# Moving the first q of the second attention, and the weight splits behind it, into the block ahead of it

## The reference

```python
h   = layernorm(x) * (1 + ca) + sa
q_c = rmsnorm(h @ w_qa, g_qa)                    # 192 wide
q   = (q_c @ w_qb) -> 32 heads, q_nope 128 | q_rope 64
kv  = h @ w_kva;  k_c = rmsnorm(kv[:64], g_kva);  k_rope = kv[64:]
k_nope, v = k_c @ w_kvb                          # per head 128 | 128
q_rope, k_rope = rope(q_rope), rope(k_rope)      # a*cos + rotate_half(a)*sin
scores  = [q_nope|q_rope] . [k_nope|k_rope] * 192**-0.5
out     = softmax(scores) @ v;  x = x + ga * (out @ w_o)
```

## Time and profile before

| | |
|---|---|
| profiled execution, its own time | 926.43 us |
| its span (first to last instruction) | 924.3 us |
| median of three timed runs | 926.45 us |
| PE busy | 823.0 us, 89% of the span |
| DVE busy | 679.4 us, 74% |
| ACT busy | 534.9 us, 58% |
| POOL busy | 536.3 us, 58% |
| granted TensorE clock, mean | 0.963 of full |

### The profile page before, as it was taken

One profiled execution on the slowest core, in us unless ns is written; L12 is line 12 of the kernel. 1 busy time (PEld: TensorE's weight loads), 2 busy tenths in 40 slices (PEclk: granted clock), 3 DMA queues, 4 the chain that ended last, 5 costly groups with the idle time before them and its releaser, 6 DMA issues.

```text
span 924.3 us, 15057 instructions
## 1 busy us (share of the span) xinstructions
PE 823.0 (89%) x4560; PEld 543.3 (59%) x4560; DVE 679.4 (74%) x1321; ACT 534.9 (58%) x1157; POOL 536.3 (58%) x480
## 2 busy tenths in 40 slices
PE   3699996399997894799999999999999999999997
PEld 1478875387775772456556565656565656565443
DVE  3639888644543562989888989899998889898662
ACT  3667884533332772666666666666566666666522
POOL 1414432112132223898888888889788888887313
PEclk9989998699999895999999999999999999999999
DMA  8360000563434340466666666666567666666511
GB/s 327 123 232 2 1 2 2 173 170 116 141 104 126 111 152 12 101 162 147 161 148 158 149 158 150 160 147 154 131 151 184 179 152 153 154 154 148 127 39 68
DMA packets 91567, 120.84 MB, mean 131 GB/s; under 512 B 30368, under 2 KB 41632, under 8 KB 91488
## 3 DMA queue, kind: packets, MB, share of 16 engines
q1 hardware_dynamic: 66912, 86.31, 33.6%
q10 hardware_dynamic: 24576, 33.59, 14.8%
HBM read 42.22 MB, written 2.10 MB: 48 GB/s over the span
## 4 chain that ended last, share of the span: by engine, by line
PE 44%; DVE 9%; issue 5%; ACTq 2%; ACT 2%; POOL 1%; DMA 0%; POOLq 0%; DVEq 0%; SPq 0%
PE bank L1451 11%; PE bank L1438 6%; PE bank L1439 4%; PE bank L1440 4%; PE bank L1465 4%; PE bank L1466 3%; PE bank L1467 3%; PE bank L1509 3%; DVE blk L1569 2%; DVE cT_lo L1643 2%; ACTq L1380 2%; DVE stage_a L1545 1%; DVE nmax L1553 1%; PE bank L1424 1%; PE bank L1425 1%
## 5 line engine op out<-in xcount | busy, mean ns | idle before, releaser
L1553 DVE TENSOR_REDUCE nmax<-bank 128x1 f32<-128x512 f32 x256 | 174.1, 680 | 46.7 <-PE bank L1440 45.5
L1715 ACT ACTIVATE prob<-bank,nmax 128x512 f32<-128x512 f32 x172 | 118.2, 687 | 109.7 <-DVE nmax L1553 97.6
L1822 POOL TENSOR_TENSOR prob<-prob,rinv 128x512 f32<-128x512 f32 x129 | 132.5, 1041 | 37.0 <-DVE rinv L1561 35.7
L1438 PE MATMUL bank<-xk_hi,q_hi 128*128 128x512 f32 x256 | 113.4, 443 | 18.5 <-ACT prob L1715 9.6
L1569 DVE STREAM_TRANSPOSE blk<-prob 128x512 f32<-128x512 f32 x172 | 120.2, 699 | 6.9 <-ACT prob L1758 5.6
L1438 PEld LDWEIGHTS bank<-xk_hi,q_hi 128*128 128x128 f32 x256 | 48.4, 189 | 96.9 <-issue 52.2
L1439 PE MATMUL bank<-xk_lo,q_hi 128*128 128x512 f32 x256 | 101.9, 398 | 0.0
L1440 PE MATMUL bank<-xk_hi,q_lo 128*128 128x512 f32 x256 | 101.0, 395 | 0.0
L1817 POOL TENSOR_TENSOR q_lo<-stage_a,q_hi 128x512 fp32r<-128x512 f32 x64 | 82.1, 1283 | 28.2 <-ACT q_hi L1709 28.1
L1813 POOL TENSOR_TENSOR stage_a<-stage_a 128x512 f32<-128x512 f32 x64 | 82.7, 1293 | 7.0 <-DMA stage_a<-stage_a 6.2
L1715 ACT ACTIVATE stage_a<-bank,nmax 128x512 f32<-128x512 f32 x84 | 57.7, 687 | 48.0 <-DVE nmax L1553 42.9
(11 more groups left out here) (242 smaller groups left out, 1940.3 us busy)
## 6 DMA issues: line engine op xcount, KB each, us to landing
pT<-blk SPq DMA_DIRECT2D x256, 64.0 KB, 2.1
pT<-blk ACTq DMA_DIRECT2D x256, 64.0 KB, 2.1
raw_e<-blk SPq DMA_DIRECT2D x256, 64.0 KB, 2.1
raw_e<-blk ACTq DMA_DIRECT2D x256, 64.0 KB, 2.1
raw_e<-in_wo SPq DMA_DIRECT2D x16, 512.0 KB, 4.0
stage_a<-stage_a SPq DMA_DIRECT2D x128, 64.0 KB, 2.0
raw_e<-in_wmod SPq DMA_DIRECT2D x6, 1024.0 KB, 11.2
stage_a<-in_wmod SPq DMA_DIRECT2D x12, 512.0 KB, 4.4
```

The lines of the kernel that those rows point to most:

```text
L1438: pe.matmul(sbk, q_hi[:, u % 2, q], xk_hi[:, 2, ks], start=True, stop=False)
L1553: dve.tensor_reduce(nmax[:, s % RING:s % RING + 1], s_bank[s % 2][:, :], AX.X, ALU.max, negate=True).then_inc(max_done, 1)
L1715: act.activation(prob[s % RING], s_bank[s % 2][:, :], ACT.Exp, bias=nmax[:, s % RING:s % RING + 1], accum_out=rsum[:, s % RING:s % RING + ...
L1822: pool.tensor_tensor(prob[s % RING], prob[s % RING], bc(rinv[:, s % RING:s % RING + 1], [P, S]), ALU.mult).then_inc(norm_pool, 1)
```

## The change

Unit 0's q is made wholly inside the preparation block, and unit 1's q up to its sum. In detail:
- The helpers of the q chain move ahead of the preparation block (`act_weights`, `pool_weights`, `pe_project`, `swap`, `rotate`, `q_round`, `q_sum`, `q_rest`), with their buffers; `qf` and `qu` lie where two of the probability buffers lay, and these where `qf` and `qu` were. The q bank becomes bank 7, which in the preparation holds the gates.
- ACT: couple 0's `w_hi` at the end of round 4, `q_round(0)` at the end of round 6, couple 1's `w_hi` at the end of round 8. POOL: couple 0's `w_lo` and the clearing of `qu` behind `nrm.lo` of tile 4, `q_sum(0)` behind that of tile 6, then `q_rest(0)`, `q_sum(1)` and couple 1's `w_lo` behind tile 7. PE: `project(0)` at the end of round 5, `project(1)` at the end of round 7. DVE: `rotate` of units 0 and 1 at the ends of rounds 5 and 7. SP: the two swaps behind the tables.
- The four gates move from rounds 3 to 6 to rounds 0 to 3.
- All of this leaves the start of the attention block, which begins with `scores(0)`, `project(2)`.

```diff
-                    return t - 3 if 3 <= t <= 6 else None
+                    return t if t <= 3 else None
...
-                        sp.wait_ge(rot_in, 64)
+                        sp.wait_ge(acc_set, 1)
+                        for u in range(2):
+                            swap(sp, u)
...
+                            if t == TPB:
+                                act_weights(act, 0)
+                            if t == TPB + 2:
+                                q_round(act, 0)
+                            if t == TILES:
+                                act_weights(act, 1)
...
                         for t in range(TILES):
                             nrm.dve_lo(pool, t)
+                            if t == TPB:
+                                pool_weights(pool, 0)
+                                pool.wait_ge(split2_lo, wc_base + KC)
+                                pool.memset(qu[:, :], 0.0).then_inc(acc_set, 1)
+                            if t == TPB + 2:
+                                q_sum(pool, 0)
+                        q_rest(pool, 0)
+                        q_sum(pool, 1)
+                        pool_weights(pool, 1)
...
+                            if t in (TPB + 1, TPB + 3):
+                                if t == TPB + 1:
+                                    dve.wait_ge(rot_in, 64)
+                                for part in range(2):
+                                    rotate(dve, (t - TPB) // 2, part)
...
+                            if t in (TPB + 1, TPB + 3):
+                                if t == TPB + 1:
+                                    pe.wait_ge(gate1_done, 4)
+                                    pe.wait_ge(xklo_done, TPB)
+                                pe_project(pe, (t - TPB) // 2)
...
-                    project(0)
-                    project(1)
                     for s in range(STEPS):
...
-                    dve.wait_ge(acc_set, 1)
-                    for u in (0, 1):
-                        for part in range(2):
-                            rotate(u, part)
...
-                    weights(0)
-                    q_round(0)
...
-                        if s == 0:
-                            weights(1)
...
-                    pool.memset(qu[:, :], 0.0).then_inc(acc_set, 1)
-                    weights(0)
-                    q_sum(0)
-                    q_rest(0)
-                    q_sum(1)
```

More of the change, by code:

```diff
@@ new lines, in megakernel, with ge, act_weights @@
+            acc_set = sem("acc_set")
+            s_ps = sem("s1_ps")
+            q_hi = sb("q_hi", [P, 2, S], F32R, ph)
+            q_lo = sb("q_lo", [P, 2, S], F32R, ph)
+            qf, qu = stage_flat[:, 0:S], stage_flat[:, S:2 * S]
+            qs = sinq[0:KVR, :]
+            q_bank = bank[7]
+            def ge(eng, s_, v):
+                if v > 0:
+                    eng.wait_ge(s_, v)
+            def act_weights(act, j):
+                ge(act, q_ps, 2 * j)
+                p = j % HP
+                act.activation(w_hi[:, :, :, :], wq_all[:, 2 * p:2 * p + 2, :, :], ACT.Copy).then_inc(whi_done, 1)
@@ new lines, in pool_weights, with pe_project @@
+            def pool_weights(pool, j):
+                p = j % HP
+                pool.wait_ge(whi_done, j + 1)
+                pool.tensor_tensor(w_lo[:, :, :, :], wq_all[:, 2 * p:2 * p + 2, :, :],
+                                   w_hi[:, :, :, :].bitcast(F32), ALU.subtract).then_inc(wlo_done, 1)
+            def pe_project(pe, u):
+                b, p, e = u // NH, u // 2, u % 2
+                ts = slice(b * S, (b + 1) * S)
+                hi, lo = w_hi[:, e, :, :], w_lo[:, e, :, :]
+                if e == 0:
+                    pe.wait_ge(wlo_done, p + 1)
+                ge(pe, qrot, 2 * u)
+                pe.matmul(q_bank[:, :], hi[:, 0, :], xk_hi[:, 0, ts], start=True, stop=False)
+                pe.matmul(q_bank[:, :], hi[:, 0, :], xk_lo[:, 0, ts], start=False, stop=False)
+                pe.matmul(q_bank[:, :], lo[:, 0, :], xk_hi[:, 0, ts], start=False, stop=False)
+                pe.matmul(q_bank[:, :], hi[:, 1, :], xk_hi[:, 1, ts], start=False, stop=False)
+                pe.matmul(q_bank[:, :], lo[:, 1, :], xk_hi[:, 1, ts], start=False, stop=True).then_inc(q_ps, 1)
@@ new lines, in q_round, with q_sum, q_rest @@
+            def q_round(act, u):
+                act.wait_ge(qsum, u + 1)
+                ge(act, s_ps, (u - 1) * TPB)
+                act.activation(q_hi[:, u % 2, :], qf[:, :], ACT.Copy).then_inc(qhi_done, 1)
+            def q_sum(pool, u):
+                pool.wait_ge(qrot, 2 * u + 2)
+                pool.wait_ge(swap_in, 32 * (u + 1))
+                pool.tensor_tensor(qf[:, :], qf[:, :], qu[:, :], ALU.add).then_inc(qsum, 1)
+            def q_rest(pool, u):
+                pool.wait_ge(qhi_done, u + 1)
+                pool.tensor_tensor(q_lo[:, u % 2, :], qf[:, :], q_hi[:, u % 2, :].bitcast(F32),
+                                   ALU.subtract).then_inc(qlo_done, 1)
@@ L1271, in megakernel @@
             prob_own = sb("prob", [P, RING - 2, S], F32, ph)
[L1272 removed]
+            prob = [prob_own[:, n, :] for n in range(RING - 2)] + [stage_flat[:, 2 * S:3 * S], stage_flat[:, 3 * S:4 * S]]
             blk = sb("blk", [P, T_SLOTS, TPB, TPB, P], F32, ph)
@@ L1385, in _ @@
                 def _(sp):
[L1386 to L1394, removed]
+                    for u in range(2, 4):
+                        swap(sp, u)
                     for u in range(UNITS):
@@ L1416, in _ @@
                 def _(pe):
[L1417 to L1428, removed]
                     def scores(s):
```

91 lines of the change are left out of this document (32 added, 59 removed).

## The result

The changed kernel takes 935.24 us (median of four runs, 932.91 to 936.43) against 927.04 of the kernel before in the same runs: ratio 1.0091, 95% interval 1.0059 to 1.0123, so 8.4 us slower by the ratio. In a second series of seven runs, beside the last experiments, it took 932.97 against 926.86, ratio 1.0062 (1.0038 to 1.0086), 5.7 us; together 6 to 8 us. The forecast was slower by 3.3 us, 929.7. The profiled execution took 936.02 us, its span 933.7, 9.4 more than before.

The account below looks back on a forecast made before the run. PE was taken to bound the preparation, unit 1's q chain the attention's entry. Stalls, project(0) and tail 17.3 us, with the clock 20.1, less 16.8 at the entry: +3.3 on 926.43, so 929.7; own range 928.3 to 931.5, 8-in-10 range 925.0 to 934.

Parts of the forecast that it names:

- gates moved: Preparation block, PE: four gates in rounds 0 to 3 instead of 3 to 6 cost 0, bounds -0.5 and +0.9 us.
- first stall: Preparation block: PE waits 4.8 us before tile 5, whose remainder on POOL stands behind couple 0's w_lo and the memset.
- second stall: Preparation block: PE waits 6.3 us before tile 7, whose remainder on POOL stands behind q_sum(0), itself waiting for tables and swaps.
- project(0) and tail at full clock: Preparation block: project(0) in round 5 adds 1.2 us on PE; the tail after tile 7's first matmul grows by 5.0 us.
- clock: PE in the preparation: clock falls in both stalls, 1.4 us for each tile, +2.8 us; bounds 0 and +4.
- start of the attention: The barrier after the preparation comes 20.1 us later: stalls, project(0) and tail 17.3, with the clock 20.1.
- barrier to round 1's row maximum: Entry into the attention: 4.9 us left of 21.65, a gain of 16.8 us, bounds 15.6 and 17.1.
- C: Rival: the same mechanism the other way, or an entry of 10 us instead of 4.9; 934 us; chance 0.14.
- side sum of 2.6 us: Table load: estimate from the Trainium skill for 256 KB, instead of 3.8 us; second stall would be 1.2 us shorter.
- A: Rival: clock holds in the first stall or both; 928.3 us with one fall, 926.9 with none; chance 0.20.
- B: Rival: attention comes into step another way; half of 9.5 us gone gives 925.0, with one clock fall less 923.6; chance 0.12.
- D: Rival: POOL's stalls don't arise because PE is late by then anyway; 915.8 us; chance 0.04.

Follow-up runs that it names:

- both places mended: Changed kernel with POOL's couple 0 w_lo and memset behind tile 5's remainder, q_sum(0) behind tile 7's, ACT's q_round(0) a round later: 920.15 us, ratio 0.9930.
- the best run: Changed kernel with POOL's waits behind the remainders, q_round(0) later, tables loaded first, couple 1's w_lo earlier, q_sum(1) behind the barrier: 912.79 us, ratio 0.9855.

## Why the prediction was right and wrong

The direction was right, and so were the two gaps, their releasers and the fall of the clock behind both; the size was not: +3.3 forecast, +8.4 and +5.7 measured. By its own terms, against the profile of after:

| term | forecast | measured |
|---|---|---|
| gates moved | 0 | -0.15 up to tile 4 (tile 0 began 0.57 later, ahead of the gates) |
| first stall | 4.8 | 4.62 (gap) |
| second stall | 6.3 | 6.18 (gap; two misses cancel, see below) |
| project(0) and tail at full clock | 1.2 + 5.0 | see below |
| clock | 2.8 | about 6.9 |
| landing of the sine table | 3.8, in the second stall | 4.5 |
| start of the attention | +20.1 | +25.4 |
| barrier to round 1's row maximum | 4.9 | 4.44 |
| new banks and places of buffers | 0 | not tested by itself |
| rest of the attention | 0 | +1.2 (within the spread of the profiles) |

The step that failed is the clock's: "at full clock each costs 0.12 less, some 1.4 us for a tile". I took the price of a tile from tile 0 and charged the twelve matmuls only. In tile 0 the clock rose while the couples' matmuls ran, so their price at half clock wasn't in the row:

```profile
308.00:309.00 1.00, 1.00 (x6) 1.00 (x5) 0.00 (x0) 0.00 (x0) 1.00 (x1) 0.50 0.09 16
309.00:310.00 1.00, 1.00 (x9) 1.00 (x7) 0.00 (x0) 0.77 (x5) 0.12 (x1) 0.79 0.00 0
310.00:311.00 1.00, 1.00 (x6) 0.23 (x5) 0.63 (x5) 0.59 (x3) 0.00 (x0) 1.00 0.00 0
```

At half clock all of PE's instructions of a round are longer: 7.01 instead of 3.79 us to `turn` is +3.2 a tile, of which the twelve matmuls are 1.5 and the couples' 1.7. The transposes of `turn` take 0.55 instead of 0.38, and project(0) takes 347.93 - 346.11 = 1.82 instead of some 1.2. Behind the first gap the couple's end, which releases the last loads, comes 3.2 us later; the 0.8 us of `turn` and project(0) fall into the wait for the tables and cost nothing. Behind the second, unit 1's rotation starts 368.48 - 358.79 = 9.7 us after tile 7's first matmul where I had 6.0, and where it was 361.35 - 355.26 = 6.1 with the gaps filled: +3.7. So the clock cost about 6.9 us for 2.8.

The attention began 5.3 us later than forecast. The clock is 4.1 of that, the later landing of the sine table 0.7, and 0.57 was there at tile 0 already. The bound that I gave the clock, +4 us, was made from the same too narrow count, and with it the forecast's own range ended at 931.5; the 934 at the end of the whole range was C's. The run with the gaps filled puts the clock's share at 4 to 7 us in the timed runs.

The terms that came from following one instruction to the next held to 0.2 us: the first gap, 3.54 from a rotation to its sum (356.25 - 352.65 = 3.60), and the sum and w_lo behind the last one (371.89 - 368.48 + 2.5 = 5.9 for 6.1). The second gap came out right by two misses that cancel: the chain from the couple's end to tile 7 took 358.79 - 345.67 = 13.1 us and not 12.4, since the table landed later, and PE's own work in it 6.9 and not 6.1, since the clock was low. How long the sine table takes to land isn't a constant here: it was 3.7 to 4.8 us in the nine profiles that load it behind the couples. The prediction's side sum of 2.6 us has no support in them; its source was on loads that GpSimd issues, and SyncE issues this one.

The 4.9 us from the barrier to round 1's row maximum rest on no row, and no run shows them. It took 4.44 us: the matmuls came some 0.43 us apart from 374.71 on, and 0.23 apart from 378.20 on.

The rivals. A, a clock that holds, is excluded: it fell behind both gaps in both profiles. B and C, another step of the attention, are excluded as causes of the 25.4 and 17.2; the rest lay between 1.8 us below and 1.2 above the kernel before's in the other eleven profiles, so no entry that was tried brought half of B's 9.5 us. C's 934 is close to what was measured, but not by its cause: the entry took 4.44 us, not 10, and the rest only 1.2 more. D fell, both gaps were there; its 915.8 was reached only with both places mended, the tables first and couple 1's w_lo ahead of the last sum.

## What to carry to other kernels

Work moved into a block with room pays for itself only if it doesn't stand ahead of something that the bound engine waits for: here three instructions of POOL, put ahead of two others of 1.27 us, made a loss of 6 to 8 us, and the same instructions behind them a gain of 7 (and with the tables' load, couple 1's w_lo and the last sum moved too, of 13). Before such a move, follow for every new wait what stands behind it on its engine, and what releases it, up to the DMA that was issued last. And a gap on TensorE costs its length and then the half clock behind it, on every instruction of the round and not only on the large matmuls: take the price from a stretch that lies wholly at the lower level (here 7.01 us for 3.79). Then see which part of it another wait hides.

## What the hardware showed that I had not expected

- A gap of 4.62 us on PE brought the clock to its lower level in every profile that had one and no filling (four more than the changed kernel's first); one of 1.77 us did not, nor did one of 3.34 us ahead of the barrier's end in the best run. Behind a gap the low level lasted so long that a tile took 5.16 to 7.01 us instead of 3.79, varying from execution to execution of the same program. The Trainium skill (TensorE: Matmul & The Clock Gate, section Why this matters for your kernels) warns of such gaps; these rows agree.
- The fp32 matmuls of the couples, with 64 to 512 columns, take nearly twice as long as well: 3.64 us for 1.94.
- One and the same 256 KB load, issued by SyncE behind the same others, landed in 3.7 to 4.8 us from profile to profile.
- Filling a gap with matmuls that do nothing useful, 65 of them, made the kernel 4 to 7 us faster.
